# Graph attention with an expert layer: edge tiles gathered once into a ring, read through registers, with half scores joined on TensorE

## The reference

```python
e = jax.nn.leaky_relu(a_src[src] + a_dst[dst], NEG_SLOPE)
m = jax.ops.segment_max(e, dst, num_segments=N)
e = jnp.exp(e - m[dst])
denom = jax.ops.segment_sum(e, dst, num_segments=N)
msg = xh[src] * (e / denom[dst])[:, :, None]
out = jax.ops.segment_sum(msg, dst, num_segments=N)
```

## Time and profile before

| | |
|---|---|
| median of 3 runs | 1910.21 us (1908.91 to 1910.95) |
| the profiled execution | 1910.08 us |
| its span in the trace | 1908.2 us |
| mean granted TensorE clock | 0.957 of full speed |
| busy: PE, DVE, ACT, POOL | 88%, 73%, 58%, 64% |

### The profile page before, as it was taken

The page is one execution under the profiler, slowest core; times in us unless marked ns, Lnnn a source line. Parts: engine busy times, 40 slices in busy tenths (PEclk is TensorE's granted clock), DMA queues, the critical chain, the costliest instruction groups (busy, mean ns, idle before and its releaser), DMA issues.

```text
span 1908.2 us, 37628 instructions
## 1 busy us (share of the span) xinstructions
PE 1676.6 (88%) x10798; PEld 1168.8 (61%) x10798; DVE 1393.3 (73%) x3802; ACT 1107.5 (58%) x2386; POOL 1216.6 (64%) x1157
## 2 busy tenths in 40 slices
PE   6679888898988989888899888946999999999997
PEld 5445554454544545445454444634989899898996
DVE  6787877877778877787778779997666666666664
ACT  3556666766667666776677666773443434434443
POOL 1377777777777777777777777302566566665553
PEclk9889999999999999999999999977999999999999
DMA  8755446455564555545555544592333333233222
GB/s 281 215 147 144 124 141 166 120 156 158 142 167 120 155 156 144 161 125 148 163 144 142 145 125 125 202 351 95 49 49 52 49 49 54 47 52 52 47 45 32
DMA packets 124147, 240.41 MB, mean 126 GB/s; under 512 B 25065, under 2 KB 82997, under 8 KB 122773
## 3 DMA queue, kind: packets, MB, share of 16 engines
q0 software_dynamic: 62800, 147.76, 32.7%
q1 hardware_dynamic: 51816, 80.51, 12.6%
q10 hardware_dynamic: 9340, 9.73, 1.5%
HBM read 195.47 MB, written 43.30 MB: 125 GB/s over the span
## 4 chain that ended last, share of the span: by engine, by line
PE 42%; POOL 29%; issue 11%; DVE 10%; DMA 6%; DVEq 0%; ACT 0%; POOLq 0%; ACTq 0%
POOL gather_ring L1136 29%; PE bank L2068 15%; PE bank L2085 14%; PE bank L1263 5%; DMA gather_ring<-node_table,src_slot 4%; PE bank L1229 3%; PE bank L720 1%; PE bank L2049 1%; DVE acc L1160 1%; DVE feat L1411 1%; DMA xT<-in_x_turned 1%; PE bank L976 1%; PE bank L1796 1%; DVE gather_ring L1188 1%; DMA raw_idx<-src_pad,edge_tile_i 1%
## 5 line engine op out<-in xcount | busy, mean ns | idle before, releaser
L1136 POOL DMA_INDIRECT gather_ring<-node_table,src_slot x879 | 838.3, 954 | 268.3 <-issue 255.1
L1229 PE MATMUL bank<-ones 128*128 128x512 bf16 x1787 | 557.6, 391 | 70.9 <-ACT gather_ring L1304 59.7
L1263 PE MATMUL bank<-gather_ring,onehot 128*128 128x264 f32 x1758 | 565.0, 404 | 56.7 <-DVE gather_ring L1188 55.7
L1263 PEld LDWEIGHTS bank<-gather_ring,onehot 128*128 128x128 f32 x1758 | 291.3, 194 | 268.9 <-DVE gather_ring L1188 232.2
L1160 DVE TENSOR_TENSOR acc<-acc,bank 128x264 f32 x879 | 369.0, 420 | 17.1 <-PE bank L1263 15.1
L1188 DVE TENSOR_TENSOR gather_ring<-gather_ring,bank 128x256 f32<-128x256 f32 x879 | 360.3, 410 | 0.3 <-ACT bank L1303 0.3
L2158 POOL DMA_INDIRECT out_rows<-y,token_idx x105 | 201.7, 1921 | 218.8 <-DMA out_rows<-y,token_idx 156.2
L1229 PEld LDWEIGHTS bank<-ones 128*128 128x128 bf16 x1787 | 170.9, 100 | 217.9 <-issue 96.9
L2127 ACT ACTIVATE hid<-bank,cols 128x256 f32<-128x256 f32 (+1 forms) x448 | 210.4, 551 | 148.1 <-PE bank L2068 145.2
L2068 PE MATMUL bank<-xe,w_hi 128*128 128x256 f16 (+1 forms) x1792 | 285.6, 267 | 1.6 <-DVE xe L1990 1.5
L2085 PE MATMUL bank<-w,hid_hi 128*128 x1680 | 278.2, 273 | 0.0
(11 more groups left out here) (316 smaller groups left out, 1963.3 us busy)
## 6 DMA issues: line engine op xcount, KB each, us to landing
w_stage<-in_L_ffn_W SPq DMA_DIRECT2D x16, 1024.0 KB, 7.0
dst_row<-dst_rows SPq DMA_DIRECT2D x110, 128.0 KB
gather_ring<-node_table,src_slot POOLq DMA_INDIRECT x879
w_split<-w_out SPq DMA_DIRECT2D x32, 256.0 KB, 3.0
w<-w_split SPq DMA_DIRECT2D x8, 1024.0 KB, 10.3
node_table<-acc ACTq DMA_DIRECT2D x24, 264.0 KB
r_ring<-in_x_lanes SPq DMA_DIRECT2D x7, 896.0 KB, 7.1
xt<-in_x_lanes SPq DMA_DIRECT2D x24, 256.0 KB, 4.7
```

Of the source, the lines that this page charges most:

```text
L1136: e.indirect_dma_start(out=gather_ring[:, b % GB, j, :], out_offset=None, in_=node_table, in_offset=bass.IndirectOffsetOnAxis(ap=src_slot[ ...
L1229: e.matmul(to[:, :].rearrange("p (k n) -> p k n", k=2), halves[:, 0:P], halves.rearrange("p (a n) -> p a n", a=1).broadcast_to([P, 2, 2 * ...
L1263: e.matmul(bank[AGG[s % len(AGG)]][:, 0:ROW], onehot[:, b % OHB, j, :], gather_ring[:, b % GB, j, :], start=True, stop=True).then_inc(summ ...
```

## The change

Each edge tile is gathered once, 832 gathers in 104 batches, and no longer once per slot. A slot finds its rows by a **place**, its number in the ring, that is worked out in stage 1 into `slot_table` and read into registers by VectorE and by TensorE (`load_places`); GpSimd reads from the same table how many messages must be made before it may write over a part of the ring, and SyncE which counts of gathers a batch needs (`landed`). Messages go to a ring of their own, 12 slots long (`MR`), and `onehot` has two buffers where it had three. The sources' half scores are no longer added on VectorE in `score` (L1173): TensorE adds them to the picked ones in PSUM, with eight products of the identity with the ring's last 8 columns (`join`), and VectorE's `sum_picks(b + 1)` waits for `join(b + 1)`. The eight filler products ahead of a batch are gone; the one ahead of each slot stays. The maxima over partitions for the expert weights are made by TensorE and VectorE (`tensor_peaks`, `vector_peaks`) where GpSimd made them, the weights W1 and W2 go through one staging buffer in 16 units of six batches, and half of the `lo` pieces are cut between a batch's messages (`vector_weights_between`). Stage 1 turns the source lists straight from a plain load. The later stages are as before.

```diff
+        message_ring = early.take("message_ring", [P, MR, ROW])
+        OHB = 2
...
-        idle_bank, IDLE_PRODUCTS = bank[5], 16
+        idle_bank = bank[5]
         gained = bank[6]
-        tile_regs = {}
-
-        w1_loaded, w2_loaded = sem("w1_loaded"), sem("w2_loaded")
-        w1_bias_done, w1_max_made, w1_top_made, w1_scaled, w1_hi_made, w1_lo_made = (
-            sem(n) for n in ("w1_bias_done", "w1_max_made", "w1_top_made", "w1_scaled", "w1_hi_made", "w1_lo_made"))
-        w2_max_made, w2_top_made, w2_scaled, w2_hi_made, w2_lo_made = (
-            sem(n) for n in ("w2_max_made", "w2_top_made", "w2_scaled", "w2_hi_made", "w2_lo_made"))
+        tile_regs, place_regs, landed_regs = {}, {}, {}
+        SPANS_AT_ONCE = 8
...
+        UNITS, UNIT_AT, UNIT_STEPS = 2 * NE, GB, 6
+        LOAD_AT, BIAS_AT, MEASURE_AT, SPREAD_AT, TOP_AT, HI_AT = 0, 2, 1, 3, 4, 4
...
-        def pool_weights(e, b):
-            ee, step = w1_step(b)
-            if step == TOP_AT and ee < NE:
-                e.wait_ge(w1_max_made, ee + 1)
-                e.partition_all_reduce(w1_top[:, ee, :], w1_max[:, ee, :], P,
-                                       bass.bass_isa.ReduceOp.max).then_inc(w1_top_made, 1)
...
+        def tensor_peaks(e, b):
+            u, step = unit_step(b)
+            if not 0 <= u < UNITS:
+                return
+            n = 2 - u % 2
+            if step == MEASURE_AT + 1:
+                e.wait_ge(max_made, u + 1)
+                e.transpose(gained[0:n, 0:P], unit_max[:, 0:n], ident[:, :]).then_inc(max_turned, 1)
+            if step == SPREAD_AT:
+                e.wait_ge(peaks_made, u + 1)
+                e.matmul(gained[:, PEAK_AT:PEAK_AT + n], ones[0:n, :], unit_peaks[0:n, 0:n], start=True, stop=True
+                         ).then_inc(peaks_spread, 1)
...
+        def vector_weights_between(e, b):
+            u, step = unit_step(b)
+            if 0 <= u < UNITS and HI_AT <= step < HI_AT + 2:
+                vector_lo(e, u, 2 * (step - HI_AT))
...
+        def load_row_of(e, row, at, n, least, most):
+            _, values = nc.values_load_multi_w_load_instructions(
+                slot_table[row:row + 1, at:at + n], engines=[e.engine], min_val=least, max_val=most,
+                skip_runtime_bounds_check_because=IN_RANGE)
+            return values
+
         def load_tiles(e, b):
-            _, values = nc.values_load_multi_w_load_instructions(
-                node_tile_row[0:1, b * EB:(b + 1) * EB], engines=[e.engine], min_val=0, max_val=NT,
-                skip_runtime_bounds_check_because=IN_RANGE)
-            tile_regs[e.engine, b] = values
+            tile_regs[e.engine, b] = load_row_of(e, TILES_AT, b * EB, EB, 0, NT)
+
+        def load_places(e, b):
+            place_regs[e.engine, b] = load_row_of(e, PLACES_AT, b * EB, EB, 0, PLACES - 1)
+
+        def row_at(e, b, j):
+            ring_rows = gather_ring[:, :, :, :].rearrange("p g j d -> p (g j) d")
+            return ring_rows[:, bass.ds(place_regs[e.engine, b][j], 1), :]
...
-            for b in batches:
-                pool_weights(e, b)
-                if b >= GB:
-                    e.wait_ge(summed, (b - GB + 1) * EB)
-                for j, s in enumerate(slots_in(b)):
+            for t in batches:
+                if t >= GB:
+                    if (t - GB) % SPANS_AT_ONCE == 0:
+                        at = t - GB
+                        spans = load_row_of(e, SPANS_AT, at, min(SPANS_AT_ONCE, TILE_BATCHES - GB - at), 1, USED)
+                    e.wait_ge(messages, spans[(t - GB) % SPANS_AT_ONCE])
+                    e.sem_inc(m_sems["passed"], 1)
+                for j, i in enumerate(tiles_of(t)):
                     e.indirect_dma_start(
-                        out=gather_ring[:, b % GB, j, :], out_offset=None, in_=node_table,
-                        in_offset=bass.IndirectOffsetOnAxis(ap=src_slot[:, s:s + 1], axis=0)
-                    ).then_inc(gathered[b % GB], 16)
+                        out=gather_ring[:, t % GB, j, :], out_offset=None, in_=node_table,
+                        in_offset=bass.IndirectOffsetOnAxis(ap=src_tile[:, i:i + 1], axis=0)
+                    ).then_inc(gathered[t % GB], 16)
...
             def sum_picks(b):
-                e.wait_ge(picks_done, b + 1)
+                e.wait_ge(joined, b + 1)
                 vector_order.of(e.tensor_reduce(picked[:, b % 2, :, :], pick_bank(b), AX.X, ALU.add))
                 vector_w1_bias(e, b)
 
             def score(b):
-                e.wait_ge(gathered[b % GB], 16 * (EB * (b // GB) + len(slots_in(b))))
-                e.wait_ge(vector_order.sem, vector_order.n)
                 if b:
                     e.wait_ge(weighed, 2 * b)
-                vector_order.of(e.tensor_tensor(zbuf[:, 0, :, :], gather_ring[:, b % GB, :, D:ROW],
-                                                picked[:, b % 2, :, 0:HEADS], ALU.add))
                 e.wait_ge(vector_order.sem, vector_order.n)
-                vector_order.of(e.scalar_tensor_tensor(zbuf[:, 1, :, :], zbuf[:, 0, :, :], NEG_SLOPE,
-                                                       zbuf[:, 0, :, :], ALU.mult, ALU.max))
+                both = picked[:, b % 2, :, 0:HEADS]
+                vector_order.of(e.scalar_tensor_tensor(zbuf[:, 1, :, :], both, NEG_SLOPE, both, ALU.mult, ALU.max))
...
             def message(b, j):
-                row = gather_ring[:, b % GB, j, 0:D].rearrange("p (h d) -> p h d", d=DH)
+                s = b * EB + j
                 if j == 0:
                     e.wait_ge(weighed, 2 * b + 1)
-                e.tensor_tensor(row, row, weights(b)[:, j, :].rearrange("p (h a) -> p h a", a=1)
-                                .broadcast_to([P, HEADS, DH]), ALU.mult).then_inc(messages, 1)
+                if s >= MR:
+                    e.wait_ge(summed, s - MR + 1)
+                e.tensor_tensor(message_ring[:, s % MR, 0:D].rearrange("p (h d) -> p h d", d=DH),
+                                row_at(e, b, j)[:, :, 0:D].rearrange("p a (h d) -> p (a h) d", d=DH),
+                                weights(b)[:, j, :].rearrange("p (h a) -> p h a", a=1).broadcast_to([P, HEADS, DH]),
+                                ALU.mult).then_inc(messages, 1)
 
             def messages_and_adds(b):
                 for j, s in enumerate(slots_in(b)):
                     message(b, j)
                     if s >= ADDS_BEHIND:
                         add(*divmod(s - ADDS_BEHIND, EB))
+                    if j == 1 and b + 1 < BATCHES:
+                        load_tiles(e, b + 1)
+                    if j == EB // 2 - 1:
+                        vector_weights_between(e, b)
+                    if j == EB - 3 and b + 1 < BATCHES:
+                        load_places(e, b + 1)
...
             e.wait_ge(acc_started, GROUPS)
+            load_tiles(e, 0)
+            load_places(e, 0)
             sum_picks(0)
             for b in range(BATCHES):
-                load_tiles(e, b)
                 score(b)
-                vector_w1(e, b)
-                vector_w2(e, b)
+                vector_weights(e, b)
...
-                                    .rearrange("p a i c -> p (a i c)"), start=True, stop=True)
+                                    .rearrange("p a i c -> p (a i c)"), start=(j == 0), stop=False)
                 made.then_inc(picks_done, 1)
+
+            def join(b):
+                load_places(e, b)
+                e.wait_ge(rows_landed, GB * (b + 1))
+                for j in range(EB):
+                    at = j * 3 * PICK
+                    made = e.matmul(bank[PICKS[b % 2]][:, at:at + HEADS], ident[:, :], row_at(e, b, j)[:, :, D:ROW]
+                                    .rearrange("p a h -> p (a h)"), start=False, stop=(j == EB - 1))
+                made.then_inc(joined, 1)
...
             picks(1)
+            join(0)
             for b in range(BATCHES):
                 if b == 0:
                     e.wait_ge(acc_started, GROUPS)
-                keep_clock(e, IDLE_PRODUCTS // 2, idle_bank)
+                if b + 1 < BATCHES:
+                    join(b + 1)
                 e.wait_ge(onehot_made, b + 1)
                 e.wait_ge(weighed, 2 * b + 2)
                 for j, s in enumerate(slots_in(b)):
-                    keep_clock(e, IDLE_PRODUCTS // 2 // EB, idle_bank)
+                    keep_clock(e, 1, idle_bank)
                     e.wait_ge(messages, s + 1)
                     if s >= len(AGG):
                         e.wait_ge(added, s - len(AGG) + 1)
-                    e.matmul(bank[AGG[s % len(AGG)]][:, 0:ROW], onehot[:, b % OHB, j, :], gather_ring[:, b % GB, j, :],
+                    e.matmul(bank[AGG[s % len(AGG)]][:, 0:ROW], onehot[:, b % OHB, j, :], message_ring[:, s % MR, :],
                              start=True, stop=True).then_inc(summed, 1)
+                tensor_peaks(e, b)
...
+            def landed(b):
+                if b % 2 == 0 and b >= GB:
```

(17 more changed lines are left out.)

473 lines of the change are left out of this document (270 added, 203 removed).

## The result

The changed kernel takes 2216.7 us (median of 4 runs, 2214.3 to 2218.7), the kernel before in the same comparison 1910.6 us (1908.9 to 1911.1): a ratio of 1.161, 95% interval 1.159 to 1.162. It is 306 us slower. The forecast was 2108 us, in a range of 2000 to 2185: the direction is right, the size 109 us too small and outside the range. Some kernels also ran on two slower chips, where even the kernel before took 2172 and 2191 us and of whose runs mainly ratios are used; a ratio compares the undisturbed runs of both kernels, while the time beside it is the median of all.

The account below looks back on a forecast made before the run. GpSimd bounded the kernel before; a loop through VectorE and TensorE would bound the changed one. 108.9 + 109 x 11.30 + 56 + 6.7 = 1403.3 us ends the edge stage, 198 us later, so 2108 us, range 2000 to 2185.

Parts of the forecast that it names:

- The loop: Edge stage, each batch waits for the chain through VectorE and TensorE of the batch ahead: 10.94 us a batch.
- The register loads: New loads: 0.59 us on TensorE, bringing the join 0.75 us after the picks; 0.40 us each among VectorE's messages.
- the join: TensorE's eight f32 products behind the picks: 0.231 us each, 1.85 us in all, bounds 1.04 and 2.58 us.
- The clock: TensorE in the edge stage: a fall in most batches, adding 0.36 us a batch, bounds 0 and 1.3 us.
- Single batches: Edge stage extras: bias products 29.6 us, `lo` pieces between messages 19.2 us, peaks' products 7.4 us, together 56 us.
- The start: Start of the edge stage: join(1) waits for `acc` at 105.15 us, first message at 108.9 us.
- The tail: End of the edge stage: 6.7 us behind the last batch's first message, as in the kernel before.
- GpSimd's pace: Gathers in the edge stage: 9.5 us a batch after the change against 10.0, a saving of 51 us if GpSimd bounds.
- No falls: Rival: small products keep TensorE's clock up, so 10.94 us a batch, 2069 us; chance 0.20.
- Two falls' worth: Rival: a slow join doubles the clock's delay, 1.3 us more a batch, 12.2 us, 2206 us; chance 0.09.
- Half covered: Rival: sequencers run ahead and hide half the load pauses, 9.9 us a batch, 1956 us; chance 0.07.
- faster: Rival: all register loads covered, 8.84 us a batch, GpSimd bounds again, 1859 us; chance 0.07.

Follow-up runs that it names:

- order alone: Changed kernel with VectorE's sum of the next batch's picks moved behind the current batch's messages and additions: 2057.4 us, ratio 1.077 to the kernel before.
- the best version: Changed kernel with that sum late, both engines' register loads moved and six filler products a batch: 1955.9 us, ratio 1.025 to the kernel before.
- the fillers: Changed kernel with three filler products ahead of the picks' load, three ahead of the join's and three behind the join: 2187.0 us, ratio 1.145 to before.
- the loads alone: Changed kernel with VectorE's two register loads a batch moved out from among its messages: 2117.4 us, ratio 1.109 to the kernel before.

## Why the prediction was right in direction and wrong in size

**The loop** (message 8, last sum, picks, join, reduction, message 1): right. It bounds the changed kernel, GpSimd waits for it, and breaking it by order alone gave 158 us. Two sums of the prediction are off by 0.1 us without effect: 8 x 1.259 is 10.1 and not 10.0, and 105.15 + 3.67 is 108.8 and not 108.9.

**The register loads**: the step that failed. "the new register load. One takes 0.59 us on TensorE's sequencer" and "so 0.40 us each" took the duration from a program with one load a batch. With two, each is 0.77 and 0.82 us and stops VectorE for 0.62 us. At full clock the loop is 11.79 us and not 10.94. The 0.85 us are 0.46 among the messages, 0.27 ahead of picks and join, put down to the loads as well (two that are 0.17 us longer each; these were not moved by themselves), and 0.12 for the join and its hand-over: 109 x 0.85 = 93 us. My upper bound for the loads among the messages (0.6 each) took the old duration too, so that it left no room for longer loads. The join of 1.85 us itself was right to 0.1 us.

**The clock**: right that it would fall in most batches (in the profiled run a fall begins in 73 of 109, and none is at 2.4 GHz throughout), at 0.36 us too little. The usual batch of the profiled run is 12.36 us, 0.57 over the loop at full clock: +23 us. This term can't be told apart cleanly from the loads. I priced a fall by a stretch of 5.34 us that was only partly at the lower level; one at it takes 6.14 us, with the loads or without them, so that among the messages either cause alone would have made most of the loss. The order in which they are counted here (loads first, clock on top) is a choice. Ahead of the picks and the join there is no such overlap.

**Single batches**: 56 us forecast, (12.71 - 12.36) x 109 = 38 us found; -18 us, perhaps since waits in such a batch overlap in part with what it adds, which was not tried. **The start**: message 1 at 117.4 us and not 108.9, +8 us: VectorE's last work of stage 1 on `acc` ends at 110.2 us and not at 105.1, VectorE stands 1.56 us ahead of the first reduction (111.78 us), where its first two register loads are, and the second join, 3.58 us long, starts only at 113.28 us. **The tail**: 7.4 for 6.7 us.

Together 93 + 23 - 18 + 8 + 1 = 107 us, and 1403.3 + 107 = 1510 us is where the stage ends. That the sum closes is no proof of its terms, since the clock and the single batches are what is left over.

**GpSimd's pace**: 9.5 us a batch, right; the best version reaches 9.59. Of the 51 us it was to save, (9.92 - 9.59) x 110 = 36 are there in the usual batch, and the long bias batches take away more than that.

**The rivals.** No falls (2069 us): refuted by the windows, and by the fillers' 28 us. Two falls' worth (2206 us) is near in time and wrong in its reason: on top of the loop at full clock the falls cost 0.57 us, not 1.3. Half covered and faster: refuted. At full clock the loop is 11.79 us and not 9.9 or 8.84, and a load in VectorE's way costs 0.38 us where it is 0.60 long, and 0.62 where it is 0.82. What these rivals had right shows in the kernel before, which carries twice the loads at no cost: loads are hidden when another engine sets the pace, and stand in the way when the loop does.

On the clock, the trace shows this: over 702 to 705 us TensorE ends a sum, makes eight picks and stands for 0.35 and 0.92 us, still at 2.4 GHz, and in the join behind them the clock falls; over 705 to 709 us TensorE is busy 3.91 of 4 us and at half speed. From 130 to 1480 us the profiled run has 105 such falls and no pause of TensorE over 1.05 us. The Trainium skill (TensorE: Matmul & The Clock Gate, "HAM oscillation — how this bites in real kernels") explains a fall by idle gaps longer than any here; by it alone the loop would have kept its clock, and the trace disagrees. On the loads, the Trainium skill (DMA: Bandwidth & Descriptors, "Latency and other measured facts") gives a floor of about 600 ns for a `tensor_load`. The traces agree for one load a batch, with medians of 590 to 598 ns; with two, each takes 0.76 to 0.82 us, which a floor doesn't rule out and doesn't foretell.

## What to carry to other kernels

An instruction that the change adds should not be priced by the old one's duration when the change also adds to their number: bound it upwards by the longest that the trace shows (822 ns in the earlier trace rows would have done here). Where a new wait goes round through two engines, write the loop down and ask first whether an order alone breaks it. A stall costs in the loop and nothing off it: the same lengthening of loads cost the kernel before nothing and this one, at full clock, 0.73 x 109 = 80 us. Where two causes cover each other, as the loads and the lower clock do between message 1 and message 8, taking out one gains little and says little of its size: 28 us for the clock alone, 98 us for the loads alone. Split the stretch by the granted clock before pricing either.

## What the hardware did that was not expected

- A register load of 8 numbers took 0.59 (TensorE) and 0.60 us (VectorE) with one load a batch, 0.76 and 0.82 us with two, whichever row or table it read, and whether the two stand 0.85 or over 3 us apart. Registers of two batches held at once don't do it (0.60). What in the second load does it stays open.
- TensorE's clock fell 105 times with no pause over 1.05 us, around picks, register loads and small f32 products, and nine fillers of 512 columns a batch brought the edge stage (200 to 1200 us) from 0.77 to 0.93.
- A join of 8 f32 products of 8 columns takes 1.95 us at 2.4 GHz, of which 1.86 us are busy with weight loads, and 3.47 us with the clock at 1.2 GHz for nearly all of it.
